# Single-input gamma and bias, and side work moved by thirds of a step, in a hand-ordered five-engine attention kernel

## What is computed

```python
x = x + 0.5 * ffn(layernorm(x), router_w, router_b, expert_w, expert_b)
x = x + attn(layernorm(x), Wq, Wk, Wv, Wo, lq1, lq2, lk1, lk2, rms_w)
x = x + 0.5 * ffn(layernorm(x), router_w, router_b, expert_w, expert_b)
```

```python
energy = jnp.where(causal, NEG, jnp.einsum('bqhad,bkhad->bahqk', qd, kd))
scores = jax.nn.softmax(energy / np.sqrt(D), axis=-1)
lam = (jnp.exp(jnp.sum(lq1 * lk1, -1)) - jnp.exp(jnp.sum(lq2 * lk2, -1)) + LAM_INIT)[None, :, None, None]
diff = scores[:, 0] - lam * scores[:, 1]
diff = jax.nn.softmax(jnp.where(causal, NEG, diff), axis=-1)
att = jnp.einsum('bhqv,bvhd->bqhd', diff, v)
att = att * jax.lax.rsqrt(jnp.mean(att * att, axis=-1, keepdims=True) + EPS) * rms_w
return (att * (1.0 - LAM_INIT)).reshape(b, s, E) @ Wo
```

## Time and profile before

| | |
|---|---|
| median of 3 runs | 1824.33 us (1821.73 to 1828.74) |
| the profiled execution | 1832.2 us, span 1830.4 us |
| busy over the span | PE 80%, DVE 79%, ACT 69%, POOL 59% |
| mean granted PE clock | 0.869 |
| main loop, 500 to 1500 us, busy | PE 895, DVE 884, ACT 828, POOL 726 us of 1000 |

### The profile page before, as it was taken

One profiled execution on the slowest core, in us unless ns is written; L12 is line 12 of the kernel. 1 busy time (PEld: TensorE's weight loads), 2 busy tenths in 40 slices (PEclk: granted clock), 3 DMA queues, 4 the chain that ended last, 5 costly groups with the idle time before them and its releaser, 6 DMA issues. The chain is left out here.

```text
span 1830.4 us, 43823 instructions
## 1 busy us (share of the span) xinstructions
PE 1465.6 (80%) x10688; PEld 1028.4 (56%) x10688; DVE 1454.8 (79%) x5505; ACT 1261.2 (69%) x3426; POOL 1084.6 (59%) x1493
## 2 busy tenths in 40 slices
PE   3996735988889898988888988888888888888620
PEld 3542313766666666666666666666666666566310
DVE  6778416888898888889988888888989877684477
ACT  2362325787788788878888888878878777675320
POOL 5421534666677777777777777777767666554300
PEclk9998866788899999989999999899989977886855
DMA  8024221111111111111111111111111100001186
GB/s 305 2 64 151 83 68 32 35 36 32 30 46 45 50 44 50 44 44 47 48 44 44 44 44 44 44 44 50 49 45 50 47 22 17 17 23 41 41 314 251
DMA packets 178954, 115.99 MB, mean 63 GB/s; under 512 B 139090, under 2 KB 139474, under 8 KB 178899
## 3 DMA queue, kind: packets, MB, share of 16 engines
q1 hardware_dynamic: 178898, 115.34, 21.4%
HBM read 50.26 MB, written 33.55 MB: 46 GB/s over the span
## 5 line engine op out<-in xcount | busy, mean ns | idle before, releaser
L1670 ACT ACTIVATE ex<-bank,nbias 128x512 f32<-128x512 f32 (+3 forms) x1024 | 528.8, 540 | 80.9 <-DVE bank L1214 78.6
L1214 DVE TENSOR_SCALAR_CACHE_REDUCE bank<-bank,nesc 128x512 f32<-128x512 f32 (+3 forms) x1024 | 503.2, 551 | 88.8 <-PE bank L1925 88.1
L1955 PEld LDWEIGHTS bank<-vs,pr 128*128 128x128 f32 x2560 | 332.8, 205 | 24.3 <-issue 12.3
L1955 PE MATMUL bank<-vs,pr 128*128 (+1 forms) x2560 | 337.6, 283 | 10.2 <-DVE att L1260 5.7
L1937 PE MATMUL bank<-cst,df 128*128 128x128 f32 x1280 | 264.6, 309 | 85.9 <-ACT pr L1687 85.2
L1923 PE MATMUL bank<-ks,hall 96*128 (+2 forms) x1024 | 266.7, 337 | 71.5 <-ACT ex L1670 48.1
L1517 POOL TENSOR_SCALAR ex<-ex,gam 128x128 f32<-128x128 f32 (+3 forms) x512 | 318.7, 635 | 0.0
L1687 ACT ACTIVATE pr<-bank 128x128 f32<-128x128 f32 (+3 forms) x512 | 232.3, 454 | 87.9 <-PE bank L1937 86.8
L1240 DVE CUSTOM_DVE_ANT_0 df<-ex 128x128 f32<-128x128 f32 (+3 forms) x512 | 261.3, 525 | 8.5 <-issue 4.0
L1937 PEld LDWEIGHTS bank<-cst,df 128*128 128x128 f32 x1280 | 168.4, 166 | 114.4 <-ACT pr L1687 99.0
L1670 ACT ACTIVATION_READ_ACCUMULATOR ex<-bank,nbias 128x1 f32 x1024 | 223.8, 219 | 0.0
(11 more groups left out here) (358 smaller groups left out, 2942.1 us busy)
## 6 DMA issues: line engine op xcount, KB each, us to landing
hall<-turned SPq DMA_DIRECT2D x360, 64.0 KB, 2.1
x_dram<-hall SPq DMA_DIRECT2D x8, 1024.0 KB, 4.9
hall<-x_dram SPq DMA_DIRECT2D x8, 1024.0 KB, 14.5
c_y<-y_dram SPq DMA_DIRECT2D x8, 1024.0 KB, 14.5
out_dram<-hall SPq DMA_DIRECT2D x8, 1024.0 KB, 4.7
hall<-in_x SPq DMA_DIRECT2D x7, 1024.0 KB, 13.8
x<-x_dram SPq DMA_DIRECT2D x28, 256.0 KB, 2.7
x_dram<-x SPq DMA_DIRECT2D x28, 256.0 KB, 2.0
```

What stands on the lines that cost most here:

```text
L1214: dve.tensor_scalar(part, part, nesc[:, 0:1], None, ALU.mult, ALU.min, accum_out=nbias[:, j, i, a:a + 1]).then_inc(bias_done.sem, 1)
L1670: ac.activation(ex[j % 4][:, a, lo:hi], energy(j, i)[:, a, :], ACT.Exp, bias=nbias[:, j, i, a:a + 1], scale=-1.0, accum_out=esum[:, j, i, ...
L1955: mm = pe.matmul(bank[:, 7, t * DV:(t + 1) * DV], pr[j % 2][:, lo + k * P:lo + (k + 1) * P], val, start=(k == 0), stop=(k == t))
```

## The change

It has three parts.

1. `gamma` no longer multiplies by `esum`, and `diff_bias` no longer handles the short tile. Each becomes an operation with one tensor input and per-row scalars (`tensor_scalar` for `scalar_tensor_tensor`). POOL's `scale` takes `esum` and `gam` as two per-row scalars instead of `gam` and the constant 1. POOL's `shift` computes `(df - dmax) * rsum` and waits for `difference(0)` instead of `diff_bias`.
2. On DVE, `diff_bias` now stands ahead of `gamma` in the step.
3. The tables of the four engines: side work moves by one to four slots, and the thirds are cut otherwise. The pair work itself keeps its order on PE, ACT and POOL; where it goes into another third, side work lands in another place between it. Most moves are on POOL, ACT and PE; on DVE only `stats` moves, from slot 18 to 17.

```diff
-                    dve.scalar_tensor_tensor(out=gam[:, j, :], in0=esum[:, j, :, 0], scalar=lam[:, ds(h, 1)],
-                                             in1=rsum[:, j, :, 1], op0=ALU.mult, op1=ALU.mult)\
+                    dve.tensor_scalar(gam[:, j, :], rsum[:, j, :, 1], lam[:, ds(h, 1)], None, ALU.mult)\
                        .then_inc(gam_done.sem, 1)
...
-                    dve.scalar_tensor_tensor(out=dbias[:, j, :], in0=dmax[:, j, :], scalar=-1.0,
-                                             in1=rsum[:, j, :, 0], op0=ALU.mult, op1=ALU.mult)\
+                    dve.tensor_scalar(dbias[:, j, 1:2], dmax[:, j, 1:2], rsum[:, j, 1, 0:1], -1.0, ALU.mult, ALU.mult)\
                        .then_inc(dbias_done.sem, 1)
...
-                            [(1, inv_sums), (1, gamma), (4, diff_bias), (3, difference(0))],
+                            [(1, inv_sums), (4, diff_bias), (1, gamma), (3, difference(0))],
...
-                        gp.tensor_scalar(ex[j % 4][:, 1, lo:hi], ex[j % 4][:, 1, lo:hi], gam[:, j, i:i + 1], 1.0,
-                                         ALU.mult, ALU.mult).then_inc(scaled.sem, 1)
+                        gp.tensor_scalar(ex[j % 4][:, 1, lo:hi], ex[j % 4][:, 1, lo:hi], esum[:, j, i, 0:1],
+                                         gam[:, j, i:i + 1], ALU.mult, ALU.mult).then_inc(scaled.sem, 1)
...
-                    dbias_done.wait(gp, at.units(1), apart_p)
+                    diff_done.wait(gp, at.units(2, 0), apart_p)
                     lo, hi = span(j, 0)
-                    gp.tensor_scalar(df[j % 4][:, lo:hi], df[j % 4][:, lo:hi], rsum[:, j, 0, 0:1],
-                                     dbias[:, j, 0:1], ALU.mult, ALU.add).then_inc(shifted_short.sem, 1)
+                    gp.tensor_scalar(df[j % 4][:, lo:hi], df[j % 4][:, lo:hi], dmax[:, j, 0:1], rsum[:, j, 0, 0:1],
+                                     ALU.subtract, ALU.mult).then_inc(shifted_short.sem, 1)
...
-                run_bodies(gp, [[(5, shift)], [(2, mask), (2, scale)], []],
+                run_bodies(gp,
+                           [[(5, shift)],
+                            [(2, mask)],
+                            [(2, scale)]],
...
-                run_bodies(pe, [[(0, energies(1)), (0, energies(0)), (7, turn_diff(1))], [(8, weigh), (6, turn_diff(0))],
-                                []],
+                run_bodies(pe,
+                           [[(0, energies(1)), (0, energies(0))],
+                            [(7, turn_diff(1)), (8, weigh)],
+                            [(6, turn_diff(0))]],
```

More of the change, by code:

```diff
@@ L1646, in closing @@
                         close_root2(q)
-                run_bodies(gp, [[(5, shift)], [(2, mask), (2, scale)], []],
-                           {1: [square], 2: [post(head_root)], 4: [post(low_heads)], 7: [prep(rope_add(0))],
-                            8: [prep(rope_low(0))], 11: [prep(rope_add(1))],
-                            14: [post(root2), prep(rope_low(1)), post(low2)], 15: [prep(rope_add(2))],
-                            19: [prep(rope_low(2))]},
-                           {18: [root], 21: [low]},
+                run_bodies(gp,
+                           [[(5, shift)],
+                            [(2, mask)],
+                            [(2, scale)]],
+                           {3: [square], 4: [post(head_root), post(low_heads)], 5: [prep(rope_add(0))],
+                            6: [prep(rope_low(0))], 11: [prep(rope_add(1))], 13: [post(root2)],
+                            14: [prep(rope_low(1)), post(low2)], 19: [prep(rope_add(2))],
+                            23: [prep(rope_low(2))]},
+                           {22: [root], 23: [low]},
                            prologue,
@@ L1888, in closing @@
                     close_y(3)
-                run_bodies(ac, [[(7, probs(1)), (0, exps(1)), (0, exps(0))], [(6, probs(0))], [(5, shift)]],
-                           {1: [prep(take_x)], 5: [high_heads], 7: [rope_high(0)], 8: [post(take_heads)],
-                            10: [prep(take_chunks(0))], 12: [rope_high(1)], 13: [high2], 15: [prep(values)],
-                            16: [post(take_x2)], 17: [rope_high(2)], 20: [prep(take_chunks(1))],
-                            21: [take_y, prep(take_chunks(2))]},
+                run_bodies(ac,
+                           [[(7, probs(1)), (0, exps(1))],
+                            [(0, exps(0)), (6, probs(0))],
+                            [(5, shift)]],
+                           {1: [prep(take_x)], 4: [high_heads], 7: [rope_high(0), post(take_heads)],
+                            11: [prep(take_chunks(0))], 12: [rope_high(1)], 14: [high2], 16: [prep(values)],
+                            17: [post(take_x2)], 19: [rope_high(2)], 20: [prep(take_chunks(1))], 21: [take_y],
+                            22: [prep(take_chunks(2))]},
                            {20: [high]},
```

13 lines of the change are left out of this document (7 added, 6 removed).

## The result

The changed kernel takes **1802.91 us**, median of 4 runs (1800.56 to 1807.81), beside 1823.88 us for the kernel before on the same chip. The ratio is 0.9885, with a 95% interval of 0.9856 to 0.9914: 1.15% faster, 21 us. The forecast was 1750 us, 74 us less. The time lies in the range and on the predicted side, but a quarter of the gain came.

A forecast was written before the change was run, and what follows sets the result against it. DVE was taken as nearest the bound, with PE setting the pace behind slow-clock stretches. Terms 45 + 16 + 18 − 5 = 74 us, taken from the median of 1824, gave 1750 us; range 1700 to 1815.

The forecast's parts named there:

- The small operations, 45 us: Gamma, bias and difference on DVE: fewer holds by POOL gain 1.9 us a body, 60 us a loop, three quarters counted.
- Without gamma's and the bias's second tensor only `difference` is held: DVE's small operations: with one tensor input, gamma and bias escape POOL's holds; this underlies the 1.9 us a body.
- DVE sets the pace and three quarters of its relief therefore count: DVE paces clear stretches, PE those behind slow ones; so 45 us of the 60 us were counted.
- PE and ACT hold the pace: Rival: DVE's gain turns into waits for PE, leaving a quarter of the 60 us; about 1795 us, chance 0.17.
- the rival built on it: Rival: two-column gamma on DVE is still held by POOL, 41 us less gain, 1791 us; chance 0.05.
- I count 0: POOL's shift: two scalars as before and a wait for difference(0), a step earlier than the bias; cost 0.
- POOL's `scale`, +1.1 us a body: POOL's scale: a second scalar adds 0.07 us, 16 times a body; POOL's 10 us of room hide it.
- The moves on PE and ACT, 16 us: PE and ACT tables: 1.19 us waits for bank 6 go in some 27 bodies, 32 us; half counted.
- The clock, 18 us: PE's clock: fewer waits remove a third of the 56 us that time at 1.2 GHz costs from 500 to 1500 us.
- `root`, 5 us of loss: POOL's root comes a step after stats, behind mask; DVE's normalise waits 0 to 0.4 us, at most 11 us.
- `scale` late (1851 us): Rival: difference on DVE waits for POOL's scale in steps 2 and 3, 81 us; 1851 us, chance 0.12.
- the rival of the recovered clock: Rival: PE's clock recovers wholly, another 38 us on top of the forecast gain; 1715 us, chance 0.12.

## Why the prediction was right or wrong

- **The small operations, 45 us: the term that failed.** Their busy time fell by 113.6 − 90.8 + 71.9 − 46.3 = 48 us, and `difference` took back 279.3 − 261.3 = 18. The 30 us left are half of the 60 that I counted, and DVE as a whole is busy for 14 us less (1440.5 for 1454.8), since `normalise` and its like grew too, from 0.59 to 0.79 us. The step that failed is "Without gamma's and the bias's second tensor only `difference` is held": it holds for the bias alone, gamma was held up to 1137 ns. The other step, that DVE sets the pace and three quarters of its relief therefore count, is not borne out either. With the new POOL and DVE tables these three operations had the whole relief, 61 us, and the kernel took 0.45% more than before. There the slow `shift` stands against it, so no run says what a microsecond of DVE is worth. That speaks for the rival *PE and ACT hold the pace* without proving it.
- **The row misread.** In the earlier trace rows I took a one-tensor operation that ended inside a POOL `scale` as not held. But the POOL row is two instructions merged, of 128 and 512 columns, which take 0.37 + 0.70 = 1.07 us undisturbed, and it shows 1.50; there POOL was the one that waited. The rule of the Trainium skill ("VectorE: DVE Perf Modes", section "Mode 2×_2P — use both read ports for one tensor") that I set aside is borne out: two columns held up to 1137 ns, one column never over 217. The condition of the rival built on it came true. That its time, 1791 us, was near the measured one is partly luck: it left `shift` at 0, the moves at 16 us and the clock at 18, and each of these was off by more than 10 us.
- **POOL's `shift`, "I count 0": wrong by 132 us of POOL's time.** I compared the number of scalars and not the operations. Under the old tables it costs 30 us on the path. What it costs under the new ones is not known, since every kernel with a fast `shift` was slower there.
- **POOL's `scale`, +1.1 us a body.** Right: 443 ns at the least for 367, and 356.8 − 318.7 = 38 us in all. That POOL's room hides it was not tested by itself.
- **The moves on PE and ACT, 16 us: right in mechanism, sized too low.** Bank 6's wait went from 70.5 to 24.7, as forecast (below 40), and the two tables are worth 29 us over the same kernel without them. I had not seen that they need POOL's new places, since ACT's `rope_high` waits for POOL.
- **The clock, 18 us: a part of it came.** From 500 to 1500 us it reads 0.92 for 0.93, but the same 21 bodies have 113 us low for 128. At 0.45 us each the 15 us less are 7. The waits for bank 6 went, but a stop ahead of the scores came, with a low stretch behind it. My own rate, 0.4, came from a body whose neighbour was 46.3 us long.
- **`root`, 5 us of loss: right in place, the wait too small.** I gave 0 to 0.4 us a body; it is 1.43. What it costs is not shown: with a quarter of it gone bodies 5 to 25 took the same time.
- **`scale` late (1851 us).** It did not happen: `difference` waited for POOL for 3.3 us in all.

The sum, redone with the ratios of the runs: operations without the subtraction +9 us, the subtraction +30, POOL's and DVE's tables −30, PE's and ACT's −29: together −20 of the 21 measured, where I had −45, 0, +5 for `root`, and −34 with the clock. Each of these steps is open by some 5 us from the intervals, and they depend on their order. What stays open is why the new tables lose 2 to 3% with a faster `shift` or the old operations. The bodies at full clock say that much of it is the clock; nothing says why the clock falls more.

One sum of the prediction was off as well: the rival of the recovered clock, 38 us below 1750, is 1712 and not 1715.

## What to carry to other kernels

When several engines are within a few per cent of each other, a stall removed on one of them may be worth nothing: here 61 us less in DVE's small operations came with no gain. Look for the waits that the freed engine's consumers have of their own before multiplying the stall by the number of bodies. Two kernels are compared over the same bodies, not over the same microseconds: over the fixed 1000 us the low clock seemed to have grown, over the same work it had shrunk. A merged row of the timeline is compared with the sum of its parts' minima before it is read as a neighbour that was not disturbed. Hand-made tables are fitted to the durations of the operations in them: change the operation and the tables together, and price each replaced operation (here `subtract` for `add`) from a row of its own.

## What the hardware showed

- On POOL a `tensor_scalar` with `subtract, mult` takes 785 ns at the least for 128 float32 columns and about 1.21 us for 256; with `mult, add` or `add, mult` it is 438 ns and 0.55 us.
- A one-tensor float32 DVE operation in SBUF over two columns was held by a POOL operation beside it until that ended (gamma, up to 1137 ns for 227; 90 of 92 long ones ended with a POOL operation), one over a single column was not (512 instructions at 217 ns or less, 256 at 215 or less). POOL's power over 16 columns, 2.9 us, held none of the 27 gammas that came 1.9 to 2.1 us after its start.
- In one kernel a microsecond at the low clock cost 0.45 us of the body, by rows of two others it is 0.65 and 0.2. Twelve products put into a stop of PE moved the low stretch to the next body; its sum over 21 bodies fell from 113 to 99 us in one kernel and from 113 to 96 in another, and neither gained time.
